# Dense expert layer of a fused attention and expert block: from 34 tiles of two halves to two passes of 34 tiles

## The chip, the core and the metric

The kernel runs on one core of one Trainium2 chip. The time is the device time of one execution in microseconds (us), as the median of several runs. TensorE (PE) multiplies, VectorE (DVE), ScalarE (ACT) and GpSimd (POOL) work element by element, SyncE (SP) issues the DMAs. Every engine runs its own list of instructions in order and they meet through semaphores.

## What is computed

The reference is one transformer block on `x` of 4 x 256 tokens with 256 channels. A two-way exponential scan (`cond`) makes the queries' input and, with other constants, the input of the expert layer; both are added to `x`:

```python
x = x + attn(cond(x, f, f, w, u, cond_512), ...)          # 16 heads of 16, softmax
x = x + ffn(cond2(x, f, f, w2, u2, cond_512), ...)
# ffn, on h of 1024 x 256
scores = sigmoid(h @ gate_w.T)                             # 64 experts
top_idx = six best of the four best groups of eight, by scores + gate_bias
topw = scores[top_idx] / (sum + 1e-20) * 2.5;  w_dense[t, e] = topw or 0
hid = relu(einsum('th,eih->tei', h, w1)) ** 2 * w_dense[:, :, None]
out = einsum('tei,ehi->th', hid, w2) + relu(h @ shared_up.T) ** 2 @ shared_down.T
```

All 64 experts are computed for all tokens, and the gate `w_dense` sets most products to zero. The changed kernel computes the same.

## The kernel before

Channels lie on the 128 partitions in two chunks (`KC = 2`), tokens along the free dimension. The first 200 us are scans and attention, batch by batch (`B = 4`), with the order of every engine written out by hand. At the end of batch 3 the expert layer begins.

The 64 experts of 64 rows each make 32 tiles of 128 rows, and the shared layer makes 2 more, so `NT = 34` tiles; tiles 0 and 1 are the shared ones. The 1024 tokens are two halves of `HT = 512`. For a tile and a half the work is a chain:

- `up` (L1259, matmuls L1266 to L1268): 6 matmuls of 512 columns into a PSUM bank. The weights and the tokens are split into a rounded part and a rest (`t_hi`, `t_lo`; `hid_hi`, `hid_lo`), and three products of the parts are summed, for each of two channel chunks.
- `rectify` on ACT (L556), then `square` on POOL (L418).
- `spread` on PE (L1357): one matmul of a selection matrix `sel` (made by `select`, L1053, on DVE) with the gates `w_ch`, which puts the gate of the row's expert on all rows of the tile, in PSUM. The shared tiles have none.
- `gated` on DVE (L1075): `act = sq * spread`, with `sq` in SBUF and the gate in PSUM.
- `round_act` on ACT (L560) makes `act_hi`, and `low_act` on DVE (L1079) the rest `act_lo`.
- `down` (L1280, matmuls L1284 to L1286): 6 matmuls that add into two PSUM banks. There are four such banks for two output chunks and two halves, held over all tiles.

For each tile the loop of PE runs `up` and `spread` of half 0, `up` and `spread` of half 1, and then both `down` of the tile before. The weights of a tile (128 x 512, 256 KB) come by one DMA (L339) into one of two buffers `raw`; ACT rounds them in two pieces of 256 columns (L552, L655) and DVE takes the rest (L960, L963). Each tile is loaded once.

The expert layer's input of a batch needs the attention of that batch: residual, logarithms, `hidden2` (L850), `hid_hi`, `hid_lo`. The gates of a batch need a chain of some 34 small DVE instructions behind `gate` (`router`, L853), then `turn_weights` on PE and `evacuate_w` on ACT. Tiles 0 and 1 are begun inside batch 3: `shared_up(0)` and `shared_up(1)` (L1332) stand between attention heads on PE, and ACT has their `rectify` there. Then the four shared pieces are interleaved with the last projection, and the loop over expert tiles starts when the gates of all batches are there.

## Time and profile before

| what | value |
|---|---|
| median of 3 runs | 434.53 us (433.73 to 434.86) |
| the profiled execution | 433.69 us |
| its span, first to last instruction | 431.9 us |
| attention of the last batch ends on PE | about 209 us |
| last matmul starts | 427.3 us |
| granted clock of TensorE, mean | 0.893 |

The profiled execution's own time is 1.8 us above its span, and 0.8 us below the median. A view by stage gives busy times; "x" is the number of instructions. PE here shows the matmuls, which are pipelined: one record of a 512-column matmul lasts 0.39 us, while the next starts 0.23 us after it. So the distance of starts is what a matmul costs. "PEld" is the loading of weights beside it. A row of a timeline has the start, the duration, the engine and line, output and inputs, the number of merged instructions and, in brackets, how long the engine was idle before it and what ended that.

### The profile page before, as it was taken

Reading aid. Unit: us, or ns where it says so; the run is one execution under the profiler, and the core shown is the slowest. Engines: PE = TensorE matmul, PEld = TensorE weight load, DVE = VectorE, ACT = ScalarE, POOL = GpSimd, SP = SyncE. Lnnn points to the kernel's source line nnn. Section 1 sums busy time; section 2 is a strip of 40 time slices with the busy share of each in tenths; the row PEclk is TensorE's granted clock in tenths of the full one; section 3 lists DMA queues with packets and bytes.
Section 4 is the critical chain, followed back from the end, with each engine's and each line's share of the span. In section 5 each row is a group of like instructions: output and inputs, shape, how many; then the busy total and the mean of one; then the engine's idle time right before and its main releaser. Section 6 shows DMA issues by size and latency. Waiting matters only on the chain.

```text
span 431.9 us, 6069 instructions
## 1 busy us (share of the span) xinstructions
PE 333.6 (77%) x1628; PEld 261.3 (60%) x1628; DVE 305.9 (71%) x658; ACT 186.8 (43%) x373; POOL 140.3 (32%) x123
## 2 busy tenths in 40 slices
PE   0014337747876786888857999999999999999995
PEld 0013225536654675665546788888888888888884
DVE  6999988995799866777567766556565565555654
ACT  4014030535261545557352555455554555545541
POOL 2608553325223002003303443443334433344331
PEclk9998555955895798899798999999999999999999
DMA  5940390850183039010100111111011101111102
GB/s 168 176 132 24 116 151 2 198 97 2 50 187 59 3 112 172 14 50 2 51 0 0 51 49 49 49 49 38 35 49 49 49 31 42 49 49 49 30 18 97
DMA packets 16947, 28.02 MB, mean 65 GB/s; under 512 B 2418, under 2 KB 10786, under 8 KB 15906
## 3 DMA queue, kind: packets, MB, share of 16 engines
q1 hardware_dynamic: 16930, 27.82, 27.7%
q8 instruction: 7, 0.11, 0.1%
q14 instruction: 10, 0.08, 0.1%
HBM read 20.81 MB, written 5.24 MB: 60 GB/s over the span
## 4 chain that ended last, share of the span: by engine, by line
issue 31%; DVE 13%; POOL 10%; PE 9%; ACT 3%; DMA 2%; POOLq 1%; DVEq 1%; SPq 0%; ACTq 0%
POOL scan L418 9%; DVE scan L1075 4%; PE ps L1182 2%; DVE mx L804 2%; DMA k_st<-qk_split 1%; PE ps L1150 1%; PE ps L1169 1%; PE ps L1212 1%; PE ps L1139 1%; ACT prob L495 1%; PE ps L1223 1%; DVE hid L850 1%; DMA qk_split<-qk_lo 0%; DVE scan L736 0%; ACT o_raw L502 0%
## 5 line engine op out<-in xcount | busy, mean ns | idle before, releaser
L418 POOL TENSOR_TENSOR scan<-scan 128x512 f32<-128x512 f32 x68 | 75.4, 1111 | 131.5 <-ACT scan L556 131.5
L1075 DVE TENSOR_TENSOR scan<-scan,ps 128x512 f32<-128x512 f32 x64 | 44.0, 687 | 60.0 <-POOL scan L418 60.0
L560 ACT ACTIVATE q_st<-scan 128x512 fp32r<-128x512 f32 x64 | 40.5, 632 | 58.8 <-PE ps L1286 52.2
L1266 PE MATMUL ps<-hid_hi,k_st 128*128 128x512 f32 (+1 forms) x140 | 55.0, 393 | 2.5 <-DVE k_st L960 2.2
L1150 PE MATMUL ps<-k_st,q_st 96*128 96x256 f32 x128 | 34.8, 394 | 27.1 <-DMA k_st<-qk_split 21.7
L1079 DVE TENSOR_TENSOR q_st<-scan,q_st 128x512 fp32r<-128x512 f32 x64 | 44.1, 689 | 16.3 <-ACT q_st L560 16.3
L556 ACT ACTIVATE scan<-ps 128x512 f32<-128x512 f32 x68 | 40.4, 598 | 33.5 <-PE ps L1268 31.6
L1284 PE MATMUL ps<-q_st,k_st 128*128 128x512 f32 x136 | 54.3, 399 | 0.6 <-POOL q_st L429 0.4
L1268 PE MATMUL ps<-hid_hi,k_st 128*128 128x512 f32 (+1 forms) x140 | 54.7, 391 | 0.0
L1267 PE MATMUL ps<-hid_lo,k_st 128*128 128x512 f32 (+1 forms) x140 | 54.6, 390 | 0.0
L1285 PE MATMUL ps<-q_st,k_st 128*128 128x512 f32 x136 | 53.9, 396 | 0.0
L1286 PE MATMUL ps<-q_st,k_st 128*128 128x512 f32 x136 | 53.1, 391 | 0.0
L804 DVE TENSOR_REDUCE mx<-ps 128x2 f32<-128x512 f32 x64 | 42.4, 684 | 11.2 <-PE ps L1150 9.9
L1150 PEld LDWEIGHTS ps<-k_st,q_st 96*128 96x128 f32 x128 | 25.9, 262 | 35.1 <-issue 12.8
L495 ACT ACTIVATE prob<-ps 128x512 f32<-128x512 f32 x64 | 36.6, 593 | 23.1 <-PE ps L1169 22.3
L1139 PE MATMUL ps<-hid,wi 128*128 128x256 f32 x64 | 20.5, 482 | 31.1 <-DVE hid L772 31.1
L1169 PE MATMUL ps<-q_st,k_st 98*128 98x256 f32 x128 | 33.1, 359 | 5.8 <-ACT prob L495 5.6
L1139 PEld LDWEIGHTS ps<-hid,wi 128*128 128x128 f32 x64 | 15.3, 248 | 34.6 <-issue 31.9
L736 DVE TENSOR_TENSOR_SCAN scan<-decay,ex 128x256 f32<-128x256 f32 x32 | 33.8, 1119 | 2.0 <-ACT ex L459 1.6
L1266 PEld LDWEIGHTS ps<-hid_hi,k_st 128*128 128x128 f32 x140 | 26.3, 188 | 8.5 <-DVE k_st L960 2.4
L1169 PEld LDWEIGHTS ps<-q_st,k_st 98*128 98x128 f32 x128 | 24.7, 234 | 11.1 <-ACT prob L495 8.7
L1284 PEld LDWEIGHTS ps<-q_st,k_st 128*128 128x128 f32 x136 | 25.8, 190 | 7.3 <-issue 1.2
(133 smaller groups left out, 542.7 us busy)
## 6 DMA issues: line engine op xcount, KB each, us to landing
clip<-in_tiles SPq DMA_DIRECT2D x34, 256.0 KB, 2.6
q_st<-qk_split SPq DMA_DIRECT2D x16, 256.0 KB, 4.8
k_st<-qk_split SPq DMA_DIRECT2D x32, 128.0 KB, 5.5
qk_split<-qk_hi SPq DMA_DIRECT2D x8, 256.0 KB, 2.1
qk_split<-qk_lo SPq DMA_DIRECT2D x8, 256.0 KB, 2.1
f_sb<-in_fT SPq DMA_DIRECT2D x4, 256.0 KB, 10.1
x_sb<-in_xT SPq DMA_DIRECT2D x4, 256.0 KB, 9.2
out<-f_sb SPq DMA_DIRECT2D x4, 256.0 KB, 2.3
```

The source lines that it names most:

```text
L418: g.tensor_tensor(sq[:, half], relu[:, half], relu[:, half], ALU.mult).then_inc(sq_ready, 1)
L804: v.tensor_reduce(mx[:, b % 2, h], bank_s(n), AX_X, ALU.max).then_inc(max_ready, 1)
L1075: TT(act[:, half], sq[:, half], bank_w(half), ALU.mult).then_inc(act_ready, 1)
L1079: TT(act_lo[:, half], act[:, half], act_hi[:, half].bitcast(F32), ALU.subtract).then_inc(act_lo_ready, 1)
L1150: last = mm(bank_s(n)[:, qt], q_st[0:MAXROW, slot(b, h // HB), h % HB, qt * P:(qt + 1) * P], k_st[0:MAXROW, slot(b, h // HB), h % HB, :], ...
L1169: last = mm(bank_t(n)[:, kt], k_st[0:MAXROW + 2, slot(b, h // HB), h % HB, kt * P:(kt + 1) * P], q_st[0:MAXROW + 2, slot(b, h // HB), h % ...
L1266: mm(bank_h(slot)[:, cols], w_hi, x_hi, start=(c == 0), stop=False)
L1267: mm(bank_h(slot)[:, cols], w_hi, x_lo, start=False, stop=False)
L1268: last = mm(bank_h(slot)[:, cols], w_lo, x_hi, start=False, stop=(c == KC - 1))
L1284: mm(acc, w_hi, act_hi[:, slot], start=first, stop=False, skip_group_check=True)
L1285: mm(acc, w_hi, act_lo[:, slot], start=False, stop=False, skip_group_check=True)
L1286: last = mm(acc, w_lo, act_hi[:, slot], start=False, stop=final, skip_group_check=True)
```

## The change

The pair (tile, half) becomes the unit of work, and the order is turned round: pass 0 runs 34 tiles over tokens 0 to 511, pass 1 runs the same 34 tiles over tokens 512 to 1023, `UNITS = 68`. In words:

- PE has no `spread`, and DVE no `select`. The gates are stored in DRAM (`gates`, one row of 1024 for each half tile, ones for the shared tiles) and each unit loads two of its rows, each broadcast to 64 partitions (64 x 512, 128 KB written each), into `spread`, which lies in SBUF (`ex`). `gated` multiplies two SBUF operands.
- Each tile's weights are loaded and split twice, once in each pass, as one piece of 512 columns. The rings of `raw`, `t_hi`, `t_lo` and `spread` have 4 places instead of 2.
- The shared tiles go the same way as the others.
- On PE unit n is `up(n)` followed by `down(n - 2)`. None of it stands inside attention any more; `up(0)` follows the last `values`. The rest of the last batch (`turn_out`, projection, gate, gates' transposes) is placed among the first 18 units (`HEAD`), and its router goes in pieces of three steps behind units 6 to 13 on DVE.
- Half 0's sums are added to `x1` on DVE after unit 37, and its store is issued with the others at the end.
- The router's last two DVE steps, a split of the weights, are gone.

The core of the diff:

```diff
+UNITS = 2 * NT
+HEAD = 18
+RING = 4
+    gates = nc.dram_tensor("gates", (NT, 2, TOK), F32, kind="Internal").ap()
...
-        raw = clip[:, 0:2].rearrange("p k c s -> p k (c s)")
-        t_hi = k_st[:, 2, 0:4].rearrange("p (k n) s -> p k (n s)", k=2)
-        t_lo = k_st[:, 2, 4:8].rearrange("p (k n) s -> p k (n s)", k=2)
+        raw = clip[:].rearrange("p k c s -> p k (c s)")
+        spread = ex[:].rearrange("p k c s -> p k (c s)")
+        t_hi = k_st[:, 2].rearrange("p (k n) s -> p k (n s)", k=RING)
+        t_lo = q_st[:, 2].rearrange("p (k n) s -> p k (n s)", k=RING)
...
+            def load_spread(half, t, k):
+                for r in range(2):
+                    sp.dma_start(spread[r * (P // 2):(r + 1) * (P // 2), k],
+                                 gates[t, r, half * HT:(half + 1) * HT].unsqueeze(0).broadcast_to([P // 2, HT])
+                                 ).then_inc(ld_spread[k], 16)
+            def store_gates(b):
+                sp.wait_ge(w_ch_ready, b + 1)
+                sp.dma_start(gates[SHARED:NT, :, tok(b)].rearrange("t r s -> (t r) s"), w_ch[:, tok(b)]).then_inc(st_gates, 16)
+            def load_unit(n, half, t, k):
+                sp.wait_ge(t_lo_ready, n - RING + 1)
+                load_raw(t, k)
+                sp.wait_ge(act_ready, n - RING + 1)
+                load_spread(half, t, k)
...
-            with pool.Fori(1, TILES) as t:
-                for half in range(2):
-                    pool.wait_ge(act_ready, 2 * (t - 1) + half + 1)
-                    square(2 * (t + SHARED) + half, half)
+            with pool.Fori(1, NT) as i:
+                for k in range(2):
+                    pool.wait_ge(act_ready, 2 * i + k - 1)
+                    square(2 * i + k, k)
...
+            with sc.Fori(0, (UNITS - 2 - HEAD) // RING) as i:
+                for k in range(RING):
+                    n = RING * i + HEAD + k
+                    rectify(n, k % 2)
+                    round_act(n - 1, (k + 1) % 2)
+                    split_hi(n + 2, (HEAD + k + 2) % RING, i + (HEAD + k + 2) // RING + 1)
...
-            def gated(n, half):
+            def gated(n, k, s, turns):
                 dve.wait_ge(sq_ready, n + 1)
-                dve.wait_ge(wb_ready, n - 2 * SHARED + 1)
-                dve.wait_ge(act_lo_ready, n - 1)
-                TT(act[:, half], sq[:, half], bank_w(half), ALU.mult).then_inc(act_ready, 1)
+                dve.wait_ge(ld_spread[s], 32 * turns)
+                if not isinstance(n, int) or n >= 2:
+                    dve.wait_ge(act_hi_ready, n - 1)
+                    dve.wait_ge(act_lo_ready, n - 1)
+                TT(act[:, k], sq[:, k], spread[:, s], ALU.mult).then_inc(act_ready, 1)
...
+            for n in range(HEAD):
+                if n > 0:
+                    low_act(n - 1, (n - 1) % 2)
+                gated(n, n % 2, n % RING, n // RING + 1)
+                split_lo(n + 2, (n + 2) % RING)
+                if n == 1:
+                    residual(B - 1)
...
+                if n >= 6:
+                    for _ in range(3):
+                        next(route_last, None)
...
-                    pe.wait_ge(hid_lo_ready, 2)
-                    pe.wait_ge(hid_hi_ready, 2)
-                    pe.wait_ge(max_ready, H * B)
-                    shared_up(0)
-                    shared_up(1)
                     shifted_scores(b, HB)
...
-            def spread(k, half):
-                mm(bank_w(half), sel[:, k], w_ch[:, half * HT:(half + 1) * HT], start=True,
-                   stop=True).then_inc(wb_ready, 1)
...
+            up(0, 0, 0, 0)
             turn_out(B - 1)
+            up(1, 0, 1, 1)
             turn_normalised(B - 1)
+            for n in range(2, HEAD):
+                up(n, 0, n % 2, n % RING)
...
+                down(n - 2, 0, n % 2, (n - 2) % RING, first=(n == 2))
+            with pe.Fori(0, (NT - HEAD) // RING) as i:
+                for k in range(RING):
+                    n = RING * i + HEAD + k
+                    up(n, 0, k % 2, (HEAD + k) % RING)
+                    down(n - 2, 0, k % 2, (HEAD + k - 2) % RING)
```

How the order moves on two engines, in the words of the two instruction lists. First PE, from the last heads of attention to the last projection. The kernel before, where L1284 to L1286 are a `down` (its tiles 0 are `shared_down(0)`):

```order
L1169 MATMUL ps<-q_st,k_st 128x256 x12
L1182 MATMUL ps<-prob,v_aug 32x256 x16
L1192 MATMUL ps<-ident,o_raw 128x128 x8
L1284 MATMUL ps<-q_st,k_st 128x512
L1285 MATMUL ps<-q_st,k_st 128x512
L1286 MATMUL ps<-q_st,k_st 128x512
```

The changed kernel, where L1256 to L1258 are an `up`:

```order
L1158 MATMUL ps<-q_st,k_st 128x256 x12
L1171 MATMUL ps<-prob,v_aug 32x256 x16
L1256 MATMUL ps<-hid_hi,k_st 128x512
L1257 MATMUL ps<-hid_lo,k_st 128x512
L1258 MATMUL ps<-hid_hi,q_st 128x512
L1181 MATMUL ps<-ident,o_raw 128x128 x8
```

Two `up`, 12 matmuls, have left the attention part and stand behind its end, around the transposes of its output.

Second DVE, the first tile of the loop's body (the instructions on registers set the counts to wait for). Before, for a tile (weights' rest, selection, rest, `gated`; a second `gated` and two `low_act` follow):

```order
L960 TENSOR_TENSOR k_st<-clip,k_st 128x256 [waits up_hi_ready]
L1101 ISA
L1053 ISA [waits wb_ready]
L1053 TENSOR_SCALAR k_st<-selval,tile_no 128x128
L1103 REGISTER_ALU
L963 TENSOR_TENSOR k_st<-clip,k_st 128x256 [waits dn_hi_ready]
L1072 ISA
L1073 REGISTER_ALU [waits sq_ready]
L1074 REGISTER_ALU [waits wb_ready]
L1075 TENSOR_TENSOR scan<-scan,ps 128x512 [waits act_lo_ready]
```

Now, for a unit (`low_act`, `gated`, `split_lo`):

```order
L1057 TENSOR_TENSOR qk_lo<-scan,qk_hi 128x512 [waits act_hi_ready]
L1047 REGISTER_ALU
L1048 ISA [waits sq_ready]
L1050 REGISTER_ALU [waits ld_spread2]
L1052 TENSOR_TENSOR scan<-scan,ex 128x512 [waits act_lo_ready,act_hi_ready]
L958 REGISTER_ALU
L959 TENSOR_TENSOR q_st<-clip,k_st 128x512 [waits t_hi_ready]
```

The selection is gone, every unit splits 512 columns of weights, and all three instructions read both operands from SBUF, where `gated` read one from PSUM.

## Rows read from the trace of the kernel before

**Rows 1.** The page: busy time and instructions of each engine over the span.

```profile
PE 333.6 (77%) x1628; PEld 261.3 (60%) x1628; DVE 305.9 (71%) x658; ACT 186.8 (43%) x373; POOL 140.3 (32%) x123
```

**Rows 2.** Busy time by stage: window, length, engines, clock, DMA share, GB/s.

```profile
200.00:220.00 20.00, 16.29 (x108) 11.17 (x100) 11.74 (x50) 10.60 (x23) 5.27 (x5) 0.83 0.10 27
220.00:240.00 20.00, 13.50 (x59) 10.51 (x60) 15.11 (x51) 7.03 (x15) 6.67 (x6) 0.91 0.04 13
...
300.00:350.00 50.00, 50.00 (x218) 40.56 (x217) 29.02 (x59) 25.28 (x50) 19.23 (x18) 1.00 0.13 43
```

**Rows 3.** Groups by line and shape, 260 to 420 us: busy, mean ns, idle before.

```profile
L418 POOL TENSOR_TENSOR scan<-scan 128x512 f32<-128x512 f32 x53 | 59.3, 1119 | 98.8 <-ACT scan L556 98.8
L1266 PE MATMUL ps<-hid_hi,k_st 128*128 128x512 f32 x107 | 42.3, 396 | 0.0
...
L1079 DVE TENSOR_TENSOR q_st<-scan,q_st 128x512 fp32r<-128x512 f32 x54 | 37.2, 689 | 14.9 <-ACT q_st L560 14.9
...
L560 ACT ACTIVATE q_st<-scan 128x512 fp32r<-128x512 f32 x54 | 34.1, 632 | 49.5 <-PE ps L1286 49.5
...
L1357 PE MATMUL ps<-w_ch,k_st 128*128 128x512 f32 x53 | 20.9, 395 | 0.0
```

**Rows 4.** Timeline of all engines in the loop, somewhat over one tile.

```profile
306.14 1.20 POOL L418 TENSOR_TENSOR scan<-scan 128x512 f32<-128x512 f32 x1 [3.34 <-ACT scan L556]
...
306.67 0.40 PE L1268 MATMUL ps<-hid_hi,k_st 128*128 128x512 f32 x1
...
307.10 0.60 ACT L556 ACTIVATE scan<-ps 128x512 f32<-128x512 f32 x1 [1.04 <-PE ps L1268]
...
307.77 1.04 POOL L418 TENSOR_TENSOR scan<-scan 128x512 f32<-128x512 f32 x1 [0.43 <-ACT scan L556]
...
309.00 0.69 DVE L1075 TENSOR_TENSOR scan<-scan,ps 128x512 f32<-128x512 f32 x1 [0.77 <-POOL scan L418]
...
312.16 1.20 POOL L418 TENSOR_TENSOR scan<-scan 128x512 f32<-128x512 f32 x1 [3.34 <-ACT scan L556]
```

**Rows 5.** Timeline of PE: attention's end, two waits, and the last microseconds.

```profile
205.49 3.64 PE L1182 MATMUL ps<-prob,v_aug 128*32 128x256 f32 x32
...
221.91 1.08 PE L1223 MATMUL ps<-gw,hid 128*128 128x64 f32 x8 [2.50 <-DVE hid L850]
...
227.13 0.50 PE L1266 MATMUL ps<-hid_hi,k_st 128*128 128x512 f32 x1 [2.23 <-DVE k_st L960]
...
424.73 0.47 PE L1284 MATMUL ps<-q_st,k_st 128*128 128x512 f32 x1 [0.29 <-DVE q_st L1079]
...
427.32 0.39 PE L1286 MATMUL ps<-q_st,k_st 128*128 128x512 f32 x1
```

**Rows 6.** Timeline of ACT: four heads' exponentials near attention's end.

```profile
202.41 2.30 ACT L495 ACTIVATE prob<-ps 128x512 f32<-128x512 f32 x4 [0.17 <-ACT w_ch L542]
```

**Rows 7.** Timeline of DVE: scans and a tiny operation, each twice.

```profile
24.11 2.43 DVE L736 TENSOR_TENSOR_SCAN scan<-decay,ekv 128x256 f32<-128x256 f32 x4
...
37.91 6.49 DVE L736 TENSOR_TENSOR_SCAN scan<-decay,ekv 128x256 f32<-128x256 f32 x4
...
195.47 1.28 DVE L936 TENSOR_SCALAR wsum<-wsum 128x2 f32<-128x2 f32 x1
...
208.38 0.17 DVE L936 TENSOR_SCALAR wsum<-wsum 128x2 f32<-128x2 f32 x1
```

**Rows 8.** Timeline of POOL in the same stretches.

```profile
39.01 3.24 POOL L371 TENSOR_TENSOR clip<-ex,f_sb 128x512 f32<-128x512 f32 x2
...
195.43 1.30 POOL L393 TENSOR_TENSOR den<-den,ex 128x512 f32<-128x512 f32 x1 [24.09 <-ACT ex L520]
```

**Rows 9.** Timeline of DVE: the `low_act` that PE waits for at the end.

```profile
423.89 0.69 DVE L1079 TENSOR_TENSOR q_st<-scan,q_st 128x512 fp32r<-128x512 f32 x1
```

**Rows 10.** Busy time by stage at the start, columns as in rows 2.

```profile
10.00:20.00 10.00, 0.00 (x0) 0.00 (x0) 10.00 (x10) 0.99 (x2) 7.67 (x5) 1.00 1.10 171
20.00:24.00 4.00, 0.00 (x0) 0.00 (x0) 4.00 (x8) 0.11 (x1) 0.00 (x0) 1.00 1.11 239
```

**Rows 11.** Issues of the weight loads on SP, ns: least, median, most.

```profile
L339 SPq DMA_DIRECT2D clip<-in_tiles x32: 332/333/361, 210.4 to 409.0; - x32
```

More of the change, by code:

```diff
@@ L326, in _ @@
                     sp.wait_ge(esum_ready, 4 * B)
-                    for i in range(2):
-                        sp.dma_start(raw[:, i, :], tiles[i]).then_inc(ld_raw[i], 16)
+                    for n in range(RING):
+                        load_raw(n, n)
                 load_rows(b, 1)
@@ L645, in _ @@
-            for k in range(2):
-                sc.wait_ge(down_done, k + 1)
-                round_shared(2 + k, k)
-            evacuate_w(B - 1)
-            def tile(t, k, split=True, up_wait=None):
-                if split:
-                    sc.wait_ge(ld_raw[1 - k], up_wait)
-                    sc.wait_ge(h_ready, 2 * t)
-                    a.activation(t_hi[:, 1 - k, 0:C], raw[:, 1 - k, 0:C], ACT.Copy).then_inc(up_hi_ready, 1)
-                if isinstance(t, int) and t == SHARED:
-                    sc.wait_ge(down_done, 2 * SHARED - 1)
-                else:
-                    sc.wait_ge(down_done, 2 * (t - 1))
-                split_down(k)
-                for half in range(2):
-                    sc.wait_ge(sq_ready, 2 * (t - 1) + half + 1)
-                    rectify(2 * t + half, half)
-                for half in range(2):
-                    sc.wait_ge(down_done, 2 * (t - 1) + half + 1)
-                    round_act(2 * t + half, half)
@@ L1077, in low_act @@
-            def low_act(n, half):
-                dve.wait_ge(act_hi_ready, n + 1)
-                TT(act_lo[:, half], act[:, half], act_hi[:, half].bitcast(F32), ALU.subtract).then_inc(act_lo_ready, 1)
-            dve.wait_ge(tile_no_ready, 1)
-            dve.wait_ge(dve_const, 4)
-            route_last = router(B - 1)
-            for n in range(5):
-                next(route_last, None)
-            dve.wait_ge(up_hi_ready, 3)
-            split_up(0)
-            for _ in route_last:
-                pass
@@ L1281, in down @@
+                    mm(bank_h(k), w_hi, x_hi, start=(c == 0), stop=False)
+                    mm(bank_h(k), w_hi, x_lo, start=False, stop=False)
+                    last = mm(bank_h(k), w_lo, x_hi, start=False, stop=(c == KC - 1))
+                last.then_inc(h_ready, 1)
+            def down(n, half, k, s, first=False, final=False):
+                pe.wait_ge(act_lo_ready, n + 1)
                 for oc in range(KC):
-                    w_hi, w_lo = (w[:, k, C + oc * P:C + (oc + 1) * P] for w in (t_hi, t_lo))
+                    w_hi, w_lo = (w[:, s, C + oc * P:C + (oc + 1) * P] for w in (t_hi, t_lo))
@@ new lines, in _ @@
+            for n in range(NT + 2, NT + 2 + RING):
+                up(n, 1, n % 2, n % RING)
+                down(n - 2, 1, n % 2, (n - 2) % RING, first=(n == NT + 2))
+            with pe.Fori(0, (NT - 2 - RING) // RING) as i:
+                for k in range(RING):
+                    n = RING * i + NT + 2 + RING + k
+                    up(n, 1, k % 2, (NT + 2 + k) % RING)
+                    down(n - 2, 1, k % 2, (NT + k) % RING)
+            for n in range(UNITS - 2, UNITS):
+                down(n, 1, n % 2, n % RING, final=(n == UNITS - 1))
```

370 lines of the change are left out of this document (153 added, 217 removed).

## The prediction

> **What bounds the kernel now.** The page [rows 1] comes first: PE is the busiest engine, with 77%, but that is an average. The busy time by stage [rows 2] shows where it is a bound. From 300 to 350 us PE is busy for all 50 us at the full clock of 2.4 GHz, while DVE has 29, ACT 25 and POOL 19. From 200 to 240 us it is busy for 30 of 40. So there are two stages: a transition in which PE waits, and a loop that PE paces. In the loop the groups by line [rows 3] have no idle time before any matmul, and all others wait, POOL longest (98.8 us).
>
> The price of a matmul is not its record of 0.39 us. The timeline [rows 4] shows the same `square` of two tiles running at 306.14 and 312.16, so a tile takes 6.02 us. It has 26 matmuls (12 `up`, 12 `down`, 2 `spread`), which makes 0.2315 us for each.
>
> **The spreads go.** 32 expert tiles x 2 = 64 matmuls x 0.2315 = 14.8 us less on the engine that paces. This is the whole direct gain.
>
> **Two `up` move.** 12 matmuls stood inside attention and now follow it: 12 x 0.2315 = 2.8 us more behind its end. What their old place gives back lies between 0 and 2.8 us. There ACT loses two `rectify` ahead of the four exponentials at 202.41 [rows 6], about 0.5 us apiece when they follow each other, and has wider splits of weights instead. The scores wait for a DMA of maxima and the gate for `hid` in any case. I take 0.6, near the low end, because ACT's other inputs stay where they are.
>
> **The transition.** PE's last `values` ends at 205.49 + 3.64 = 209.1, its last matmul is done with at 427.32 + 0.23 = 427.55 [rows 5]. Of these 218.4 us, 868 matmuls of the expert layer are 200.9. Transposes, last projection and gates, which both kernels have, are some 5.7 by their records. That leaves 11.8 us of waits and slow clock, for instance 2.50 before the gate and 2.23 before the first expert tile [rows 5], both for the last batch's chain and its router.
>
> In the changed kernel pass 0 needs only batches 0 and 1, so that chain no longer stops PE by itself. But its steps are queued on ACT and DVE between the steps of the units. Walking the first 18 units through with the durations of the rows gives these stalls:
> - Start of the pipeline and the steps of the last batch (`residual`, logarithms, `hidden2`) ahead of the next `low_act`: 2.4 us.
> - Units 6 to 13 carry three router steps each on DVE, about 1.1 us a unit, on top of three 0.61 us operations and the blocks by POOL (below). That is 3.4 us a unit where PE needs 2.78: 8 x 0.6 = 5.0 us.
> - Half 0's two additions, 2 x 0.69 us, at the change of pass: 1.0 us.
> - The end: `down(67)` needs its own chain. A `rectify`, `square`, `gated`, `round_act` and `low_act` in a row are 0.6 + 1.04 + 0.69 + 0.63 + 0.69 [rows 3, 4] and about 0.7 for the handovers, 4.4 us, with only two `down` (2.8 us) beside it: 1.6 us, where before it was 0.29 [rows 5].
>
> **The loop.** Now 12 matmuls make a unit: 2.78 us. The other engines must fit in it. ACT has three operations of 0.60 to 0.63 us, 1.9 at most, and POOL one square of 1.12 [rows 3]. DVE has three of 0.69, of which the next starts 0.61 after it. Taken apart all fit. But the rows show that DVE and POOL exclude each other. Four scans take 2.43 us alone and 6.49 while POOL works, 0.61 and 1.62 apiece [rows 7], and POOL's operations beside them also take 3.24 / 2 = 1.62 [rows 8]. A tiny DVE operation of 0.17 us took 1.28 when it started 0.04 after POOL's at 195.43 [rows 7, 8]. So one POOL operation with two different inputs adds 1.01 to 1.11 us to DVE's. A square has one input and a record of 1.04 [rows 4] instead of 1.30 [rows 8], so I give it 0.75 to 1.01. Before, `gated` read PSUM and started beside a square. Now all three read two SBUF operands. One unit costs the pair 3 x 0.61 + (0.75 to 1.01) = 2.58 to 2.84 us, and with bare records up to 3 x 0.69 + 1.12 = 3.19.
>
> The chain to PE is as tight. From the end of `up`, that is 306.67 + 0.23: 0.20 to `rectify`, 0.67 to the square [rows 4], some 0.95 until it lets DVE go, 0.69 for the `low_act` of the unit before, and 0.15 to PE, as from 423.89 + 0.69 to 424.73 [rows 5, 9]. That is 2.66, or 2.74 with one more wait in `rectify`, against 2.78. I take 2.82 a unit: PE's 2.78 and 0.04 for what does not fit. It is nearest to the paired scans, which show the cost of handing over itself. For the 50 units behind the head that is 2.0 us.
>
> The Trainium skill states the same exclusion in "SBUF — State Buffer", section "Who interferes with whom": a VectorE instruction with two SBUF inputs contends with a GpSimd instruction that reads SBUF, and the later one fully blocks. This speaks against the change, since it moves `gated` into that class; the trace agrees (0.17 against 1.28 us). If "fully" is taken by whole records, the unit becomes 3.19 and the sum that of the first rival.
>
> **The transfers.** A unit moves 256 KB of weights and 2 x 128 KB of gates, 524,288 bytes in 2.82 us: 186 GB/s, where the loop has 43 [rows 2]. At the start the engines held 171 GB/s with short rows and on-chip fills, and 239 with loads alone [rows 10]. These are the bounds; I take the second, as the unit has nothing but loads, so it hides. Four ring places start each load some three units before its use. SP spends 0.33 us on an issue [rows 11], so three are 1.0 of 2.82.
>
> **The sum.** Stalls: 2.4 + 5.0 + 1.0 + 1.6 + 2.0 = 12.0, against 11.8 before. So -14.8 + 2.8 - 0.6 + 0.2 = -12.4 us. On the span 431.9 becomes 419.5, and the profiled execution's 433.69 becomes 421.3. The median lies 0.8 higher, so I forecast **422 us**. The stalls may come out 4 lower or 7 higher: 414 to 429.
>
> **The rivals.**
> 1. *DVE and POOL become the bound*, and the kernel is slower. Each unit of the loop costs the whole records, 3.19 instead of 2.82: 50 x 0.37 = 18.5, and some 4 in the head: 444 us. It decides for slower from 2.82 + 12.4 / 50 = 3.07 us a unit. For it: the margin is 0.2 us or less by every count. Against it: the paired scans hand over without loss. Chance 0.12. Half of it, a unit of 2.95 to 3.05, gives 429 to 433: 0.10.
> 2. *The transfers bound the loop.* At 171 GB/s a unit is 3.07 us: 422 + 12.5 = 434 to 438 with the head. Against it: 239 GB/s in pure loads. 0.05.
> 3. *The router is dear.* If most of its small steps meet a square and pay 1.0 us each, as the one at 195.47 did, units 6 to 13 cost twice the loss: 422 + 5 to 8 = 427 to 430. Chance 0.09.
> 4. *The exchange doesn't bring the spreads' time*, since something else paced the loop. The rows exclude it: no idle time before any matmul [rows 3].
>
> **How the numbers follow.** The forecast has 0.64 (of it 0.05 for less than 414), the rivals 0.36. The range of 8 in 10 leaves out 0.05 below 414 and about 0.13 above 435. About 0.3%, 1.3 us, is what a measurement can tell from no change. Slower by more is rival 1 and half of rival 2, 0.15; within it lies the rest of 2 and the edge of the halfway case, 0.05; faster 0.80.
>
> **What would show it.** In the loop: 12 matmuls of PE in 2.78 to 2.85 us, with small idle times before L1267 (`down`) put down to DVE. Rival 1 shows longer records on DVE and POOL, PE idle in every unit, and the cycle well above 2.9. Rival 2 shows `gated` or the split waiting for a DMA. The head shows in the stretch 210 to 260 us. My forecast is wrong most likely if the cycle is: each 0.1 us of it is 5 us of the time. A falling clock would add to that; it stood at 0.91 in the transition [rows 2], where PE idled.

## The result and the profile after

The changed kernel takes 422.4 us, the median of 4 runs (421.0 to 422.9), against 434.7 us for the kernel before (4 runs, 433.7 to 435.4). The ratio is 0.971, with a 95% interval of 0.968 to 0.975. The profiled execution took 422.82 us, with a span of 421.0. Medians, here and below, leave out executions over 1.5% above their kernel's fastest: 558.2 us of e9, 428.1 of e12, and 425.3 of e7, which is e7's profiled one.

The page of the changed kernel, busy time and instructions over the span, answers to [rows 1]:

```profile
PE 320.3 (76%) x1552; PEld 246.8 (59%) x1552; DVE 340.1 (81%) x625; ACT 201.3 (48%) x373; POOL 133.1 (32%) x116
```

By its share DVE is now the busiest engine. Whether it is the bound is read from the busy time by stage, with the columns of [rows 2]:

```profile
200.00:220.00 20.00, 18.62 (x107) 12.64 (x107) 11.26 (x47) 10.46 (x21) 4.49 (x4) 0.70 0.31 96
220.00:240.00 20.00, 16.89 (x75) 12.56 (x74) 14.66 (x21) 10.74 (x21) 4.88 (x5) 1.00 0.42 132
240.00:260.00 20.00, 18.79 (x78) 13.91 (x77) 19.51 (x54) 11.65 (x20) 8.01 (x7) 1.00 0.54 161
300.00:350.00 50.00, 50.00 (x218) 40.55 (x217) 42.72 (x57) 31.52 (x54) 18.85 (x18) 1.00 0.60 190
```

In the loop (last line) PE is busy for all 50 us, and DVE has 7 us to spare. From 240 to 260 us, where DVE carries the router beside the units, it is DVE that is full (19.51 of 20) and PE that waits. From 200 to 220 us PE is busy almost all the time, but at a mean clock of 0.70, where the kernel before had 0.83 [rows 2]. This mean mixes two levels: over the last `values` below the granted clock is 0.50 (1.2 GHz), from 213 us on it is 1.00 (2.4 GHz). They are called the lower and the upper level from here on.

The groups by line and shape, 260 to 410 us, answer to [rows 3]. L1057 is `low_act`, L457 the square, L959 the weights' rest, L1052 `gated`:

```profile
L1057 DVE TENSOR_TENSOR qk_lo<-scan,qk_hi 128x512 fp32r<-128x512 f32 x54 | 59.0, 1092 | 23.3 <-ACT qk_hi L591 23.3
L457 POOL TENSOR_TENSOR scan<-scan 128x512 f32<-128x512 f32 x54 | 56.6, 1048 | 95.6 <-ACT scan L584 95.6
...
L959 DVE TENSOR_TENSOR q_st<-clip,k_st 128x512 fp32r<-128x512 f32 x53 | 35.9, 678 | 1.5 <-ACT k_st L577 1.5
L1052 DVE TENSOR_TENSOR scan<-scan,ex 128x512 f32<-128x512 f32 x53 | 35.9, 678 | 0.0
```

`low_act` lasts 1.09 us, where it lasted 0.69 [rows 3]. The other two have 0.68. A piece of the timeline of all engines shows why, in the order start, duration:

```profile
320.27 1.04 POOL L457 TENSOR_TENSOR scan<-scan 128x512 f32<-128x512 f32 x1 [1.80 <-ACT scan L584]
...
320.75 1.11 DVE L1057 TENSOR_TENSOR qk_lo<-scan,qk_hi 128x512 fp32r<-128x512 f32 x1 [0.53 <-ACT qk_hi L591]
...
321.79 0.68 DVE L1052 TENSOR_TENSOR scan<-scan,ex 128x512 f32<-128x512 f32 x1
...
322.97 1.04 POOL L457 TENSOR_TENSOR scan<-scan 128x512 f32<-128x512 f32 x1 [1.66 <-ACT scan L584]
```

`low_act` starts 0.48 us after a square has, and comes out 0.42 longer. `gated` begins after the square is over.

The timeline of PE, answering to [rows 5]: the last `values`, the first `up` behind them, the longest wait of the head, the two last waits and the last matmul.

```profile
207.72 3.64 PE L1171 MATMUL ps<-prob,v_aug 128*32 128x256 f32 x32
211.29 0.79 PE L1256 MATMUL ps<-hid_hi,k_st 128*128 128x512 f32 x1
...
263.76 0.38 PE L1221 MATMUL ps<-ident,wful 128*64 128x128 f32 x2 [2.29 <-DVE wful L948]
...
413.22 0.50 PE L1267 MATMUL ps<-qk_hi,k_st 128*128 128x512 f32 x1 [0.98 <-DVE qk_lo L1057]
...
415.21 0.50 PE L1267 MATMUL ps<-qk_hi,k_st 128*128 128x512 f32 x1 [0.34 <-DVE qk_lo L1057]
...
416.47 0.40 PE L1269 MATMUL ps<-qk_hi,q_st 128*128 128x512 f32 x1
```

The waits of PE from 205 us on, grouped (total, times, longest), name one engine:

```profile
PE ps L1267 <- DVE qk_lo L1057: 4.3, 6, 1.5
PE ps L1221 <- DVE wful L948: 2.3, 1, 2.3
PE ps L1256 <- DVE q_st L959: 2.0, 4, 0.8
```

For the comparisons below the execution is cut in two at the end of PE's last `values`: here 211.4 us of attention, and 205.3 us from there until the last matmul is done with (416.47 + 0.23). The kernel before had 209.1 and 218.4. To see where PE stands still in the second part, the distances between the starts of its matmuls are taken where they exceed 0.3 us, less 0.23 each: 5.5 us up to 240 us, 4.8 from 240 to 262, 0.2 from there to the end of the loop (the change of pass among it), 1.8 in the last 10 us. Together 12.4.

### The profile page after: what moved, and what is told of

Same layout as the page of the kernel before. It is cut to its first block, busy times and chain, and to the rows that moved or that the text cites. A ratio compares the mean times of both kernels' runs of the same rounds, so it can differ in the third digit from the quotient of the medians.

```text
span 421.0 us, 6016 instructions
## 1 busy us (share of the span) xinstructions
PE 320.3 (76%) x1552; PEld 246.8 (59%) x1552; DVE 340.1 (81%) x625; ACT 201.3 (48%) x373; POOL 133.1 (32%) x116
## 4 chain that ended last, share of the span: by engine, by line
PE 46%; DVE 12%; issue 3%; ACT 3%; DMA 2%; POOL 1%; DVEq 0%; SPq 0%; ACTq 0%
PE ps L1256 6%; PE ps L1258 6%; PE ps L1267 6%; PE ps L1257 6%; PE ps L1268 6%; PE ps L1269 6%; PE ps L1171 3%; DVE q_st L959 2%; DVE scan L1052 2%; DVE mx L806 2%; PE ps L1139 1%; DMA k_st<-qk_split 1%; PE ps L1158 1%; DVE qk_lo L1057 1%; PE ps L1128 1%
## 5 line engine op out<-in xcount | busy, mean ns | idle before, releaser
L457 POOL TENSOR_TENSOR scan<-scan 128x512 f32<-128x512 f32 x68 | 73.1, 1076 | 138.3 <-ACT scan L584 138.3
L1057 DVE TENSOR_TENSOR qk_lo<-scan,qk_hi 128x512 fp32r<-128x512 f32 x68 | 69.3, 1020 | 30.6 <-ACT qk_hi L591 30.6
L1267 PE MATMUL ps<-qk_hi,k_st 128*128 128x512 f32 x136 | 54.5, 400 | 4.5 <-DVE qk_lo L1057 4.3
L1256 PE MATMUL ps<-hid_hi,k_st 128*128 128x512 f32 x136 | 54.4, 400 | 2.0 <-DVE q_st L959 2.0
L577 ACT ACTIVATE k_st<-clip 128x512 fp32r<-128x512 f32 x68 | 42.8, 631 | 24.4 <-PE ps L1269 24.4
L1258 PE MATMUL ps<-hid_hi,q_st 128*128 128x512 f32 x136 | 53.8, 395 | 0.0
L1257 PE MATMUL ps<-hid_lo,k_st 128*128 128x512 f32 x136 | 53.4, 393 | 0.0
L1268 PE MATMUL ps<-qk_lo,k_st 128*128 128x512 f32 x136 | 53.3, 392 | 0.0
L1269 PE MATMUL ps<-qk_hi,q_st 128*128 128x512 f32 x136 | 53.2, 391 | 0.0
L959 DVE TENSOR_TENSOR q_st<-clip,k_st 128x512 fp32r<-128x512 f32 x68 | 48.7, 717 | 1.7 <-ACT k_st L577 1.7
L1052 DVE TENSOR_TENSOR scan<-scan,ex 128x512 f32<-128x512 f32 x68 | 46.2, 679 | 0.2 <-DVE o_tok L826 0.2
L591 ACT ACTIVATE qk_hi<-scan 128x512 fp32r<-128x512 f32 x68 | 42.4, 624 | 2.7 <-DVE scan L1052 2.6
L1128 PEld LDWEIGHTS ps<-hid,wi 128*128 128x128 f32 x64 | 14.9, 244 | 34.3 <-issue 31.8
## 6 DMA issues: line engine op xcount, KB each, us to landing
f_sb<-in_fT SPq DMA_DIRECT2D x4, 256.0 KB, 10.3
```

Of the source, the lines that this page charges most:

```text
L457: g.tensor_tensor(sq[:, k], relu[:, k], relu[:, k], ALU.mult).then_inc(sq_ready, 1)
L959: TT(t_lo[:, k], raw[:, k], t_hi[:, k].bitcast(F32), ALU.subtract).then_inc(t_lo_ready, 1)
L1052: TT(act[:, k], sq[:, k], spread[:, s], ALU.mult).then_inc(act_ready, 1)
L1057: TT(act_lo[:, k], act[:, k], act_hi[:, k].bitcast(F32), ALU.subtract).then_inc(act_lo_ready, 1)
L1256: mm(bank_h(k), w_hi, x_hi, start=(c == 0), stop=False)
L1257: mm(bank_h(k), w_hi, x_lo, start=False, stop=False)
```

## Experiments

Each kernel is the changed one with the edit shown. Single times of one kernel lie up to 5 us above its median here and up to 3 below, and the kernels were measured in different groups of runs, so the stretch behind attention, read from the profile, is given beside every median. e3, e4 and e5 ran twice, the changed kernel and e12 four times, the others six times.

| kernel | median, us | ratio to before (95%) | attention ends | behind it | PE's gaps behind it: to 240, to 262, later, end |
|---|---|---|---|---|---|
| the changed kernel | 422.4 | 0.971 (0.968 to 0.975) | 211.4 | 205.3 | 5.5, 4.8, 0.2, 1.8 |
| e9_changed_again | 419.6 | 0.966 (0.961 to 0.972) | 212.1 | 205.3 | 5.6, 4.8, 0.2, 1.8 |
| e1_ups_back | 419.4 | 0.963 (0.958 to 0.968) | 205.7 | 207.8 | 10.3, 4.5, 0.1, 1.9 |
| e2_filler | 420.0 | 0.963 (0.958 to 0.968) | 208.9 | 206.5 | 5.9, 5.0, 1.0, 1.9 |
| e3_pool_twice | 454.2 | 1.042 (1.034 to 1.050) | 207.0 | 240.0 | 5.9, 4.6, 33.2, 2.8 |
| e4_pool_memset | 421.4 | 0.967 (0.960 to 0.973) | 209.8 | 205.1 | 5.6, 4.9, 0.1, 1.8 |
| e5_extra_mm | 430.2 | 0.987 (0.980 to 0.994) | 206.9 | 217.5 | 5.9, 5.3, 0.9, 1.6 |
| e6_late_weights | 419.0 | 0.961 (0.956 to 0.966) | 212.1 | 203.4 | 5.5, 2.4, 0.4, 1.9 |
| e7_no_gate_loads | 420.0 | 0.963 (0.958 to 0.968) | 212.2 | 207.2 | 5.7, 2.5, 3.9, 1.9 |
| e8_act_square | 413.7 | 0.949 (0.944 to 0.954) | 210.5 | 198.8 | 3.5, 1.0, 0.0, 1.4 |
| e12_act_square_pool_blocks | 421.3 | 0.969 (0.963 to 0.975) | 209.0 | 205.7 | 5.9, 4.5, 0.2, 1.9 |
| e10_combined | 412.9 | 0.949 (0.945 to 0.954) | 211.1 | 196.1 | 2.1, 0.1, 0.0, 1.4 |
| e11_combined_ups | 408.3 | 0.941 (0.936 to 0.946) | 206.7 | 195.4 | 3.4, 0.1, 0.0, 1.4 |

### Does PE pace the loop, and is a matmul worth 0.23 us there?

`e5_extra_mm` puts one matmul into each unit of the two counted loops:

```diff
                     up(n, 0, k % 2, (HEAD + k) % RING)
+                    mm(ps[:, 6 + k % 2, :], hid_hi[:, 0, 0:P], hid_hi[:, 0, 0:HT], start=True, stop=True)
                     down(n - 2, 0, k % 2, (HEAD + k - 2) % RING)
```

> From the changed kernel, one more matmul of 512 columns in each unit of PE's two counted loops (16 and 28 units, 44 matmuls), into a PSUM bank that nobody reads; it is a spread put back, without its result. Theory, PE paces the loop and a matmul costs 0.2315 us: 44 x 0.2315 = 10.2 us more, 432.6 us. Rival, the pair DVE and POOL is as near a bound as PE (2.77 us a unit) and hides part of it: 0 to 5 us more.

Behind attention it takes 217.5 us, 12.2 more than the changed kernel. 44 matmuls at 0.2315 are 10.2 of them. Of the other 2.0, 1.4 stand in PE's gaps (13.7 against 12.3 by the table), and most of those are clock: behind the same wait of 2.29 us before `turn_weights` its matmuls run at the lower level for some 3 us, as these two of them in its timeline of PE show (0.63 us, 0.43 apart), where in the changed kernel they last 0.40 us and start 0.23 apart.

```profile
259.02 0.38 PE L1221 MATMUL ps<-ident,wful 128*64 128x128 f32 x2 [2.29 <-DVE wful L948]
...
260.81 0.63 PE L1256 MATMUL ps<-hid_hi,k_st 128*128 128x512 f32 x1
261.24 0.63 PE L1257 MATMUL ps<-hid_lo,k_st 128*128 128x512 f32 x1
```

The median, 430.2, is 2.4 us below the expected 432.6 and 7.8 above the changed kernel's 422.4. Both of its runs are that low, and its profiled attention ended 4.4 us earlier, so the stretch behind attention decides here and not the median. Nothing in the loop hid the added work. PE paced the loop before as well [rows 2], so the 64 matmuls taken away are worth 14.8 us at this price, an estimate, since no run takes them away alone.

### Do DVE and POOL exclude each other, and how dear is it?

`e3_pool_twice` gives POOL a second product in the last 48 units, `e4_pool_memset` a write without a read:

```diff
                     square(n, k % 2)
+                    g.tensor_tensor(prob[:, k], ekv[:], ekv[:], ALU.mult)     # e3
+                    g.memset(prob[:, 2 * k:2 * k + 2], 0.0)                   # e4
```

> From the changed kernel, POOL does one more product of 512 columns in each of the last 48 units (it reads one SBUF tensor twice, as the square does, and writes memory that nobody reads). Theory, DVE's and POOL's SBUF reads exclude each other: a unit costs the pair 3 x 0.61 + 2 x (0.75 to 1.01) = 3.3 to 3.85 us where PE needs 2.78: 48 x (0.55 to 1.07) = 26 to 51 us more, 449 to 473 us, with PE idle in each unit. Rival, no exclusion, the longer low_act records come from elsewhere: POOL has 2 x 1.08 = 2.16 us of work in 2.78 and the extra product follows the square, so 422.4 us within 1.5.

> From the changed kernel, POOL writes zeros over 128 x 1024 unread columns (about 0.9 us by its one memset of 1024 columns in the profile) behind the square in each of the last 48 units: as long as a second square, but with no read of SBUF. Theory, the exclusion is one of reads: DVE's records stay (low_act 1.09, gated 0.68 us) and the time is 422.4 us within 1.5. Rival, any SBUF access of POOL excludes DVE's two-operand instructions: the same 26 to 51 us more as with a second product.

The groups by line of `e3_pool_twice`, 300 to 400 us. L470 is the added product, L457 the square, L1063 `low_act`, L965 the weights' rest and L1058 `gated`:

```profile
L470 POOL TENSOR_TENSOR prob<-ekv 128x512 f32<-128x512 f32 x29 | 42.6, 1469 | 0.0
L1063 DVE TENSOR_TENSOR qk_lo<-scan,qk_hi 128x512 fp32r<-128x512 f32 x28 | 37.4, 1337 | 4.3 <-ACT qk_hi L597 4.3
L457 POOL TENSOR_TENSOR scan<-scan 128x512 f32<-128x512 f32 x29 | 32.9, 1134 | 26.8 <-ACT scan L590 26.8
L965 DVE TENSOR_TENSOR q_st<-clip,k_st 128x512 fp32r<-128x512 f32 x29 | 32.3, 1115 | 0.0
L1058 DVE TENSOR_TENSOR scan<-scan,ex 128x512 f32<-128x512 f32 x29 | 31.5, 1087 | 0.0
```

And of `e4_pool_memset`, the same stretch, `low_act`, `gated`, the weights' rest and the added memset:

```profile
L1063 DVE TENSOR_TENSOR qk_lo<-scan,qk_hi 128x512 fp32r<-128x512 f32 x37 | 41.0, 1107 | 15.8 <-ACT qk_hi L597 15.8
L1058 DVE TENSOR_TENSOR scan<-scan,ex 128x512 f32<-128x512 f32 x36 | 24.4, 678 | 0.0
L965 DVE TENSOR_TENSOR q_st<-clip,k_st 128x512 fp32r<-128x512 f32 x36 | 24.4, 678 | 0.0
...
L470 POOL MEMSET prob<- 128x1024 f32 x37 | 35.3, 955 | 0.0
```

With the second product every DVE operation is longer, POOL's are too, and the kernel is slower than the one before. The stretch behind attention grew by 34.7 us, 0.72 for each of 48 units: a unit takes 2.77 + 0.72 = 3.5 us. If it is 3 x 0.61 of DVE and two holds by POOL, a hold (the time by which a POOL instruction delays DVE) is 0.84 us. Single records of e3's timeline say the same: a held one lasts 1.52 us, one that isn't held 0.68.

```profile
321.90 1.52 DVE L965 TENSOR_TENSOR q_st<-clip,k_st 128x512 fp32r<-128x512 f32 x1
...
324.79 0.68 DVE L1058 TENSOR_TENSOR scan<-scan,ex 128x512 f32<-128x512 f32 x1
```

This lies inside the 0.75 to 1.01 of the prediction and is shorter than the square's record of 1.05. With one square the pair needs 1.83 + 0.84 = 2.67 us, 0.1 less than PE's 2.77. So the loop fits, and the first rival missed it by little: its cause is real, its price was too high.

The memset keeps POOL busy for 0.96 us a unit more and changes no DVE record and no time: `low_act` is held by the square as before, and `gated`, which starts while the memset runs, keeps its 0.68 us. What excludes is POOL's reading. The Trainium skill says the same in "SBUF — State Buffer", section "Who interferes with whom": two SBUF inputs of VectorE contend with a GpSimd instruction that reads SBUF, not with one that only writes it. The traces agree, with 1.34 and 1.11 us for `low_act` in the two kernels. By the same section the later instruction "fully blocks"; by whole records that would be 1.05 us, and the 0.84 of these traces decides.

### Which part of the waits is the exclusion's?

`e8_act_square` moves the square from POOL to ACT. `e12_act_square_pool_blocks` is e8, with a product on POOL that nobody waits for:

```diff
             for n in range(HEAD):
                 rectify(n, n % 2)
...
                 if n > 0:
                     round_act(n - 1, (n - 1) % 2)
+                square(n, n % 2)          # ACT: a.activation(sq[:, k], relu[:, k], ACT.Square)
                 split_hi(n + 2, (n + 2) % RING, (n + 2) // RING + 1)
...
+            def block(n, k):              # POOL, e12 only
+                pool.wait_ge(relu_ready, n + 1)
...
+                g.tensor_tensor(prob[:, k], ekv[:], ekv[:], ALU.mult).then_inc(scrap, 1)
```

> From the changed kernel, the square of every unit is done by ACT (one more activation, behind round_act) and POOL does nothing in the expert layer. Theory: DVE is blocked no more, so low_act falls from 1.09 to 0.68 us; the loop stays at PE's 2.78 us a unit and gains nothing; units 6 to 13 carry three router steps on DVE and lose 1 to 3 us of their 4.4 us of waits: 419.5 to 421.5 us. Rival: ACT with four operations, 4 x 0.52 to 0.62 = 2.1 to 2.5 us of 2.78, and its extra ones for the last batch becomes the queue that PE waits for: 424 us or more.

> From e8_act_square (413.7 us), where ACT makes the squares: POOL does one product of 512 columns a unit again, at the time of the former square, from SBUF memory that does not change into memory that nobody reads. Nobody waits for it. Theory, the 6.4 us which e8 won behind attention came from POOL's reads that block DVE: low_act is back at about 1.09 us and most of them come back, 418 to 421 us, with the waits of PE between 240 and 262 us back from 1.0 to 3 or more. Rival, they came from the shorter chain (one handover less between rectify, square and gated): 413.7 us within 1.

Busy time by stage of `e8_act_square`, columns as in [rows 2]:

```profile
240.00:260.00 20.00, 19.21 (x85) 15.34 (x84) 17.89 (x56) 14.86 (x28) 0.00 (x0) 1.00 0.55 193
300.00:350.00 50.00, 50.00 (x218) 40.70 (x217) 35.96 (x57) 39.02 (x73) 0.00 (x0) 1.00 0.62 189
```

And the groups of `e12_act_square_pool_blocks`, 260 to 400 us, `low_act` and POOL's product:

```profile
L1074 DVE TENSOR_TENSOR qk_lo<-scan,qk_hi 128x512 fp32r<-128x512 f32 x50 | 58.8, 1176 | 18.8 <-ACT qk_hi L605 18.7
L465 POOL TENSOR_TENSOR prob<-ekv 128x512 f32<-128x512 f32 x50 | 52.3, 1045 | 89.5 <-ACT scan L591 89.5
```

e8 is 413.7 us, below everything I expected, and 5% under the kernel before. Its loop is as long as before, as expected: DVE has 36.0 of 50 us instead of 42.7, and nobody needed it. The gain is all in the head and the end: the stretch behind attention is 6.5 us shorter, and the gaps fall from 12.4 to 6.0 (2.0 up to 240 us, 3.8 to 262, 0.4 at the end). e12 loses the whole of it again, 205.7 us behind attention and 421.3 in the median, although ACT still makes the squares and nobody waits for POOL. So it was not the shorter chain. It was POOL's reading, which delays DVE's steps for the last batch and its router, and the single `low_act` that PE waits for at the end.

### Is the wait before `turn_weights` a wait of its own?

`e6_late_weights` moves the last batch's `turn_weights` (PE) and its evacuation (ACT) from unit 14 to unit 16.

```diff
-                if n == 14:
+                if n == 16:
                     turn_weights(B - 1)
...
-                if n == 14:
+                if n == 16:
                     evacuate_w(B - 1)
```

> From the changed kernel, the last batch's turn_weights on PE and its evacuation on ACT stand at unit 16 instead of 14. Theory: PE's longest idle time behind unit 6, 2.3 us before turn_weights for DVE's last router step, goes, and DVE has caught up with the router by then: 1.5 to 2.3 us less, 420 to 421 us. Rival: DVE is what is late there, and the same 2 us show up before the next `down`: 422.4 us, within 0.4.

The 2.29 us are gone and came back nowhere: 203.4 behind attention, 2.0 less. The median, 419.0, lies 1 us below what was expected, by less than single times spread. So of the changed kernel's 4.8 us of gaps between 240 and 262 us half belong to the place of `turn_weights`; 2.4 stay when it moves.

### Do the doubled transfers cost anything?

`e7_no_gate_loads` drops the loads of gates behind unit 3:

```diff
             def load_unit(n, half, t, k):
                 sp.wait_ge(t_lo_ready, n - RING + 1)
                 load_raw(t, k)
-                sp.wait_ge(act_ready, n - RING + 1)
-                load_spread(half, t, k)
...
-                dve.wait_ge(ld_spread[s], 32 * turns)
+                dve.wait_ge(ld_spread[s], 32)
```

> From the changed kernel, the gates are loaded for the first four units only, and all later units multiply by what lies in those four places (the output is another). The DMA traffic of the expert layer is about halved (by bytes written, 256 of 512 KB a unit), and SP issues one DMA a unit instead of three. Theory: the transfers and their issues are hidden: 422.4 us within 0.5. Rival: they take write bandwidth of SBUF from the engines or delay the weights: 1 to 4 us less, with shorter records on DVE, ACT or POOL in the loop.

The loop of `e7_no_gate_loads` by busy time, then its `turn_weights` and the second matmul behind it on PE's timeline:

```profile
300.00:350.00 50.00, 50.00 (x218) 40.52 (x217) 42.60 (x57) 31.71 (x55) 18.87 (x18) 1.00 0.32 94
```

```profile
264.81 0.61 PE L1219 MATMUL ps<-ident,wful 128*64 128x128 f32 x2 [2.29 <-DVE wful L946]
...
265.64 0.63 PE L1266 MATMUL ps<-qk_lo,k_st 128*128 128x512 f32 x1
```

Half the traffic, 94 GB/s instead of 190, and every engine has the same busy time to 0.2 us in 50. The transfers are hidden. The median of 420.0 is below my bound of 421.9. Its interval overlaps that of the changed kernel run again, so the times don't tell them apart, and the engines' records in the loop show no gain. The 207.2 us behind attention are longer than the changed kernel's 205.3 because this execution, as those of e2 and e5, came out of the wait of 2.29 us at the lower level of PE's clock (0.63 us a matmul), and the changed kernel's at the upper.

### What did the two `up` inside attention do?

`e1_ups_back` puts them back and takes them out behind attention, `e2_filler` puts 12 matmuls without use in their place and leaves the two `up` behind attention:

```diff
                 else:
+                    pe.wait_ge(hid_lo_ready, 2)
+                    pe.wait_ge(hid_hi_ready, 2)
+                    pe.wait_ge(max_ready, H * B)
+                    up(0, 0, 0, 0)        # e1; in e2 six matmuls into bank_h(0)
+                    up(1, 0, 1, 1)        # e1; in e2 six matmuls into bank_h(1)
                     shifted_scores(b, HB)
                     shifted_scores(b, HB + 1)
```

> From the changed kernel (422.4 us), the first two `up` put back inside attention on PE, ahead of the last batch's shifted scores 8 and 9. ACT and DVE keep their order. Theory, the clock: with 12 matmuls of 512 columns there, PE stays busy, its clock stays at the upper level longer, and the last `values` ends at about 209 us instead of 211.2; the 2.8 us of matmuls are gone from behind it too: 3.5 to 5 us less, 417.5 to 419 us. Rival, the moved work alone: the attention ends where it does now or 0.6 us later, and only the 2.8 us move: 2.2 to 2.8 us less, 419.6 to 420.2 us.

> From the changed kernel, 12 matmuls of 512 columns whose result nobody reads are added on PE at the place where the kernel before had its two `up` (ahead of shifted scores 8 and 9); the real two `up` stay behind attention. The output is the same. Theory, the clock: the attention ends about 2 us earlier than at 211.2, although PE does 2.8 us more work: 420 to 421 us. Rival, the later end of attention came from ACT's or DVE's order and not from the clock: the filler fills idle time or delays the scores, 422.4 to 423.5 us.

> The changed kernel once more, beside the other three of this group. In seven profiled executions whose attention part is the same code, PE's last `values` ended between 206.9 and 212.2 us, as the granted clock of its last 32 matmuls was at the upper level (1.9 us for them) or the lower (3.6 us). Theory: where attention ends is a matter of the single execution, and behind it the time is steady: 205.3 us from there to the last matmul within 0.5, whatever the end is, and a median of 419.5 to 422.5 us. Rival: the late end belongs to the changed order (its PE idles before those heads), then this one ends at 211 us or later again.

The last `values` on PE's timeline, first of e2, then of e1 with what follows it:

```profile
206.98 1.93 PE L1171 MATMUL ps<-prob,v_aug 128*32 128x256 f32 x32
```

```profile
203.80 1.93 PE L1171 MATMUL ps<-prob,v_aug 128*32 128x256 f32 x32
206.24 1.09 PE L1181 MATMUL ps<-ident,o_raw 128*128 128x128 f32 x8 [0.51 <-ACT o_raw L528]
210.48 1.09 PE L1191 MATMUL ps<-ident,o_tok 128*128 128x128 f32 x4 [3.15 <-DVE o_tok L826]
```

To take out where the attention of one execution stands as a whole, I count from the first `values` of the last batch (194.16 us in the changed kernel's profile) to the end of its last. The same code is in ten profiles (all but e1, e2 and e11):

| kernels | that stretch, us | second `values` of four | last two |
|---|---|---|---|
| before, two `up` in it | 15.6 | upper level | lower |
| changed attention code, four profiles (e3, e4, e5, e12) | 14.9 | lower level | upper |
| the same, six profiles (changed, e6 to e10) | 16.3 to 17.2 | lower level | lower, or partly |
| e1, e2, e11, with 12 matmuls more in it | 12.9 | upper level | upper |

PE does 2.8 us more work in the last line and needs 2.0 to 4.3 us less. In e2 nothing reads the result of these matmuls, and the granted clock differs as the times do: from the gates' matmuls to the end of the second `values` it is 0.50 in the changed kernel and 1.00 in e2. Without the 12 matmuls PE stands idle for 1.80 and 1.45 us until an exponential of ACT is done, and the gates' matmuls right behind (L1212) are already slow, 1.80 us for 8 records, against 1.08 in [rows 5]. PE's timeline of the changed kernel there:

```profile
197.04 0.47 PE L1158 MATMUL ps<-q_st,k_st 98*128 98x256 f32 x2 [1.80 <-ACT prob L521]
198.96 0.79 PE L1158 MATMUL ps<-q_st,k_st 98*128 98x256 f32 x2 [1.45 <-ACT prob L521]
199.55 1.80 PE L1212 MATMUL ps<-gw,hid 128*128 128x64 f32 x8
```

Whether the clock is back for the last 32 records (1.93 us, or 3.64) differs between executions of the same code. e9 ended attention at 212.1, but e5 at 206.9. So my theory for e9 holds behind attention (205.3 again) and for the median (419.6), and neither theory is right as a whole: the slow second `values` belongs to the order, in all ten, and the slow last two to the single execution. Of the kernel before there is one profile, with the last two slow; how much of the 2.0 to 4.3 us the moved `up` cost against it on average isn't shown. The Trainium skill tells in "TensorE: Matmul & The Clock Gate", section "Part 1: The HAM clock gate", that low clock is the state without activity and that the time of the switch varies between runs; the ten profiles agree.

Why, then, is e1 no faster than 419.4? Behind attention it has 12 matmuls fewer, which makes 202.6 from 205.3, and takes 207.8. There is the new wait of 3.15 us. DVE and POOL of e1 at that time:

```profile
206.78 2.06 DVE L948 TENSOR_SCALAR wful<-wsel,wrec 128x64 f32<-128x64 f32 x2
208.77 0.25 DVE L824 RECIPROCAL rsum<-ps 128x16 f32<-128x16 f32 x1
```

```profile
206.75 2.04 POOL L457 TENSOR_TENSOR scan<-scan 128x512 f32<-128x512 f32 x2 [6.84 <-ACT scan L584]
```

The last two steps of the third batch's router took 2.06 us instead of 0.41, since the squares of both early units ran in a row beside them. The normalisation stood behind, and PE behind that, with nothing left to do. In the changed kernel `up(1)` covers the normalisation. So the 2.8 us of the two `up` behind attention were not pure cost, as my sum had it. They filled a wait: e1, which doesn't have them there, loses 5.2 us in its place.

### A version that beats both

`e10_combined` is e8 with the late `turn_weights` of e6, and with ACT's logarithms, reciprocal and rounding of `hid` (units 3 to 5) behind the unit's own three activations. `e11_combined_ups` adds the two `up` of e1, and fills the wait that they open:

```diff
             turn_out(B - 1)
-            up(1, 0, 1, 1)
+            up(2, 0, 0, 2)
             turn_normalised(B - 1)
...
+            split_lo(2, 2)
             normalise(B - 1)
```

> A version meant to beat both: e8_act_square, with the last batch's turn_weights and its evacuation at unit 16, and ACT's logarithms, reciprocal and rounding of hid for the last batch (units 3 to 5) behind the unit's round_act, square and split instead of ahead of round_act. Theory: PE's waits of 1.07 and 1.08 us before two `down` at 224.7 and 228.5 and of 1.18 before turn_weights in e8 go: 2 to 3 us less than e8's 413.7, 410.5 to 412 us. Rival: the delayed logarithms hold DVE, which waits for them ahead of low_act, and the same waits come one unit later: 413 to 414 us.

> e10_combined, with the first two `up` inside attention as in e1_ups_back, and with up(2) between turn_out and turn_normalised on PE (its weights' rest is made on DVE ahead of the normalisation). Theory: in e1 the two `up` inside attention were paid for by a wait of 3.15 us before turn_normalised, which they had covered; with up(2) in that wait, 1.4 us of it are filled: 1.5 to 2.8 us less than e10, 408 to 410.5 us. Rival: the chain of ACT and DVE for the first units sets the start and not PE's amount of work: the same as e10 within 0.7.

e10's stretch behind attention is 2.7 us shorter than e8's, as expected, but its median, 412.9, only 0.8, and lies above the 410.5 to 412 expected; the two are of different groups of runs, and single times spread by more than the difference. e11 takes 408.3 us, 11.3 less than the changed kernel run beside it (e9) and 6% less than the kernel before. From the first `values` of the last batch to the last matmul it needs 12.9 + 195.4 = 208.3 us, against 16.6 + 196.1 = 212.7 in e10 and 222.5 in the changed kernel. Most of its step over e10 (3.7 of 4.4) is in attention, where the clock stays up. Behind attention it has 2.8 us of matmuls less than e10 and gains only 0.7: PE waits 1.30 us before `up(2)`, which so fills less of the wait than I expected.

## Where the prediction was right and where not

The forecast was 422, the measured median 422.4. Step by step, on the spans:

| step | predicted, us | measured, us |
|---|---|---|
| 64 spreads less | -14.8 | not apart; e5's 44 matmuls back: +12.2, of it 10.2 at 0.2315 each |
| end of attention | 208.5 | 211.4 (206.9 to 212.2 in ten profiles) |
| waits, start of the pipeline and last batch's steps | 2.4 | 5.5 |
| router units | 5.0 | 4.8 |
| change of pass | 1.0 | 0.2, with the loop |
| loop | 2.0 | see above |
| end | 1.6 | 1.8 |
| behind attention, whole | 218.4 - 14.8 + 2.8 + 0.2 = 206.6 | 205.3 |

**Right** were the gain and where it comes from, and the end. The sum of the waits was 12.0, and is 12.4 by gaps; counted as the prediction counted them before, as what is left beside 816 matmuls and 5.7 us (205.3 - 188.9 - 5.7), it is 10.7.

**Right by luck** was the number for the router's units, 5.0 against 4.8. That POOL's reading causes most of it is shown: 4.8 us with it, 1.0 without. But the 3.4 us of DVE a unit are not the sum of their parts: 3 x 0.61 + 1.1 = 2.93, and with a hold of 0.75 to 1.01 a unit is 3.7 to 3.9, which would leave 7 to 9 us. In the trace the eight units from the `gated` of unit 6 (239.06 us) to that of unit 14 (264.14) take 3.14 us each, and 2.77 in e8. By e6 the units themselves cost PE 2.4 us; the other half is the wait before `turn_weights`, for which the prediction has no term.

**The step that failed** is the 0.6 us by which attention should end earlier. I argued with ACT's inputs and did not ask what PE's clock does when 2.8 us of matmuls leave a stretch in which it waits. There was a hint in [rows 5]: the last 32 records took 3.64 us even before, where e1 and e2 have 1.93. By e2 the 12 matmuls make the stretch 2.0 to 4.3 us shorter, their own time already paid. The end came at 211.4 instead of 208.5.

**Mis-sized** were two terms that cancelled. The start of the pipeline lost 5.5 instead of 2.4: on ACT the last batch's steps stand ahead of `round_act`, and one of them waits for DVE itself. PE's two longest waits there, and the reciprocal (L550) ahead of `round_act` (L591) of unit 3 on ACT:

```profile
226.76 0.50 PE L1267 MATMUL ps<-qk_hi,k_st 128*128 128x512 f32 x1 [0.73 <-DVE qk_lo L1057]
231.32 0.50 PE L1267 MATMUL ps<-qk_hi,k_st 128*128 128x512 f32 x1 [1.52 <-DVE qk_lo L1057]
```

```profile
229.39 0.63 ACT L550 ACTIVATE den<-den 128x512 f32<-128x512 f32 x1 [1.85 <-DVE den L1079]
229.92 0.61 ACT L591 ACTIVATE qk_hi<-scan 128x512 fp32r<-128x512 f32 x1
```

I had counted these steps as work, not as waits in a queue. e10, which puts them behind the unit's own and has no square on POOL, is down to 2.1. And the loop with the change of pass lost 0.2 instead of 3.0. For the loop I took the unit as 2.82 us, near the end of 2.58 to 2.84; by e3 the pair needs 2.67. The chain to PE, which I put at 2.66 to 2.74, fits as well: in the loop no `up` or `down` waits for DVE by over 0.1 us.

**The rivals.** The first has the right mechanism. It decides from a second reading of POOL in each unit, as e3 shows with 454 us. The second is excluded by e7: half the traffic gives the same loop. The third is partly true: small router steps do pay for squares (2.06 for 0.41 us in e1), within the 5.0 that the sum already held. The fourth is excluded for the changed kernel's loop by e5, and for the loop before by PE's 50 of 50 us [rows 2]. The issues on SP were dearer than I said, some 0.35 for the weights and 1.15 for the two gates, 1.5 of 2.77 us instead of 1.0, and nobody waited for them.

**Two slips.** The range is not worked out right: 4 us below 422 is 418 and not 414, and the chances are reckoned with 435 as the upper bound, where the sum has 429; 422.4 lies inside by any of them. And the 0.17 against 1.28 us that the prediction gives as its trace of two SBUF inputs are of an instruction with one SBUF tensor; the rows of two SBUF inputs are the scans, 0.61 against 1.62 us [rows 7], and after the change `low_act`.

That 422 was met to 0.4 us is in part luck, since attention came out 2.9 longer and the rest 1.3 shorter than said in the profiled execution, and single times of one kernel spread by more.

## What to carry to other kernels

When work is moved out of a stretch in which PE waits, look at the granted clock there: PE's idle time is cheap only as long as the matmuls that follow it stay at the upper level, and useful work moved in may cost less than nothing. When a DVE operation changes from one PSUM operand to two SBUF operands beside a reading POOL, count DVE's operations plus POOL's hold against the bound; a loop may just fit, while the places without slack (the head, the end, chains of small steps) pay in full. If ACT has room, it is the better place for such a square.
